# Starting the expert stage inside the attention's tail: last z, its output projection and a router among the first chunks, buffers laid out anew, big experts first

## The chip, the core and the metric

The kernel runs on one core of a Trainium2 chip. The metric is the device time of one execution in microseconds (us); the median of three runs is compared. The core's engines are TensorE (PE in the profile, which loads weights as PEld), VectorE (DVE), ScalarE (ACT), GpSimd (POOL) and SyncE (SP, which here only issues DMAs). Each runs its own list of instructions in order and waits on semaphores for the others.

## The reference

One transformer block with adaptive layer norms, for 4 batches of 512 positions and 256 features: causal attention with 16 heads of 128, then a feed-forward part with 8 experts, 2 of which each position uses.

```
h = _layernorm(x) * (1 + ca) + sa
x = x + ga * attention(h)              # q, k, v, causal softmax, output projection W_O
h = _layernorm(x) * (1 + cb) + sb
x = x + gb * ffn(h)

# ffn: HID = [128, 256, 384, 512, 128, 256, 384, 512]; gelu is the exact one
h      = x @ down_w + down_b                               # 256 -> 128
logits = x @ router_w + router_b - 1e-7 * cost
probs  = softmax(logits); topv, topi = top_k(probs, 2); gate = softmax(topv)
for k in range(2):                                         # every expert sees h times its mask
    acc = sum over e of gelu(gelu(h * mask[e]) @ w1 + b1) @ w2 + b2
    out = out + acc * gate[k]
out = out + 0.1 * (gelu(gelu(h) @ shared_w1 + shared_b1) @ shared_w2 + shared_b2)
out = out @ up_w + up_b + gelu(x) @ core_w + core_b
```

## The kernel before, in words

Two functions write out the whole program by hand as one list of events, `attention_plan()` and then `ffn_plan()`. Every engine walks this same list and issues, in its order, the instructions that are its own. So the list sets the order on every engine at once, and an event that an engine has to wait for holds up all that stands behind it on that engine. Every float32 product is made of three matmuls (L711 to L713) of a high and a low half: ACT writes the high half (a cast or an activation), DVE the low half (a subtraction that reads PSUM), and PE needs both.

The attention runs over 64 units (4 head groups x 4 batches x 4 heads; `NU` is 64). For unit u: **q/u**, **k/u** and **v/u** project, **S/u** makes the scores, **ri** and **norm** the softmax, **ty** transposes the probabilities on DVE (L1114 to L1117), **tr** moves them by DMA, **pt** splits them (casts on ACT, L681; two subtractions on POOL, L567), and **z/u** multiplies them by v. **wo/p/c** is the output projection of a pair of units (p from 0 to 31, two halves c): PE makes 12 matmuls of 256 columns, DVE scales into `fb` (L1127), POOL adds to X (L560).

Around it lie the events that prepare the second half for batch b: **st** and **nm** are the layer norm (**st/n**, **nm/n** with n = 4 + b, on DVE; its power of -0.5 on POOL, L507), **h2/b/k** transposes it on PE and ACT and DVE split it; **r/b** is the router's matmul (16 small ones, L832 and L833), **rs/b/1** to **rs/b/14** are the router's small steps on DVE (L947 to L981) with the exponentials **rp** on POOL (L542), and **wt/b** transposes the gates on PE (L890), after which SP stores them and **wl** loads each gate's row back, spread over the partitions. **dn/b** is the down projection with its gelu (`ur`), and **wh/n** splits a piece n of weights into W (cast on ACT, L628; subtraction on POOL, L552, or for the pieces in `BY_V`, 21 and 22 among them, on DVE, L1017).

The expert stage runs over 84 chunks, 21 for each batch t: chunk 0 is the shared expert, chunks 1 to 20 are blocks of 128 hidden units of the experts. Step n issues **w1/n** (PE into one of three S banks, gelu twice on ACT, L704 and L705, low half on DVE into `Gr`, L1241), then **w2/n-3** (PE accumulates into one of two T banks), then what the table `at` puts at this step. When the last chunk of an expert is through, **acc/t/e** multiplies by the gate on DVE (L1196, into `prod`) and adds on POOL (L533). w1/n waits for the low half of chunk n-3, and the first w2 of an expert waits for the acc of the expert two before it. At the turn of the batches **gx** (gelu of the features), **hs** (a POOL addition, L575), **up** and **D** are woven in.

The list ends its attention part with h2/1/1, S/63 and the rest of unit 63's softmax, z/61, then rs/0/13, rs/0/14, r/1, wt/0, wo/30/0, the statistics and normalisation of batch 2 (st/6, nm/6), z/62, dn/0, wo/30/1 and z/63. wo/31 stands in steps 1 and 2 of the expert stage.

The buffers of the attention (`qk`, `PB`, `vh`, `vl`, `pth`, `ptl`, `zt`) give their place to those of the expert stage (`ur`, `Gr` and so on), which are laid over them.

Of the kernel before, what the change touches and what calls it, by code (L numbers as in the profile page):

```python
# [44 lines left out]
def attention_plan():  # L45

    pre, post = {}, {}
    fill = {}

    def put(where, i, *events):  # L50
        where.setdefault(i, []).extend(events)

    put(post, 0, ("ms",))
    for b in (1, 2, 3):
        i = (0, 2, 5)[b - 1]
        if b == 1:
            put(pre, i, ("h", b, 0))
            put(post, i, ("h", b, 1))
            continue
        fill[i] = [[("st", b, 0)], [("st", b, 1)], [("st", b, 2)], [("st", b, 3)]]  # L60
        fill[i + 1] = [[("nm", b, 0)], [("nm", b, 1)]]
        put(post, i + 1, ("h", b, 0))
        put(post, i + 2, ("h", b, 1))
    for n in range(4, 16):
        put(pre, 16 * (n // 4 - 1) + 5 + 2 * (n % 4), ("wh", n))
    for n in range(16, 20):
        put(pre, 34 + n, ("wh", n))
    for b in range(2):
        fill[54 + 4 * b] = [[("st", B + b, k)] for k in range(4)]
        fill[55 + 4 * b] = [[("nm", B + b, 0)], [("nm", B + b, 1)]]  # L70
        put(post, 55 + 4 * b, ("h2", b, 0))
        put(post, 56 + 4 * b, ("h2", b, 1))
        put(post, 57 + 4 * b, ("r", b))
    fill[58] = [[("rs", 0, 1), ("rs", 0, 2)]] + fill[58]
    put(post, 58, *[("rp", 0, c) for c in range(4)])
    fill[59] += [[], [("rs", 0, 3)], [("rs", 0, 4)]]
    fill[60] = [[("rs", 0, k)] for k in range(5, 10)]
    fill[61] = [[("rs", 0, k)] for k in range(10, 15)]
    put(post, 61, ("wt", 0))
    fill[62] = [[("st", 6, 0), ("st", 6, 1)], [("st", 6, 2)], [("st", 6, 3)], [("nm", 6, 0), ("nm", 6, 1)]]  # L80
    put(post, 61, ("wh", 20), ("ld", 22))
    plan = [("mod0",)] + [("st", 0, k) for k in range(4)] + [
# [11 lines left out]
    for i in range(NU):  # L94
# [36 lines left out]
def ffn_plan():
# [12 lines left out]
    for k in range(3):
        put(0, 2 + k, ("d0", k))
    put(0, 4, ("h2", 2, 0))
    put(0, 5, ("h2", 2, 1), ("wl", 2), ("wl", 3))
    for k, j in enumerate((6, 7, 8, 9)):
# [12 lines left out]
    for b, n in ((1, 5), (2, 26), (3, 47)):  # L161
# [54 lines left out]
def build(nc, x, ct, wmod, wat, wfa, wfb, cst, bcol, b2, ub, cb, out, scr, scw):  # L216
# [20 lines left out]
    with ExitStack() as ctx:  # L237
# [33 lines left out]
        with ExitStack() as att:  # L271
# [14 lines left out]
        gob = sb("gob", 256)
# [145 lines left out]
        def _(sp):  # L432
# [16 lines left out]
            for ev in plan:  # L449
# [148 lines left out]
        def _(act):  # L598
# [15 lines left out]
            for ev in plan:  # L614
# [704 lines left out]
```

## Time and profile before

| | us |
|---|---|
| median of three runs | 830.65 (829.01 to 832.02) |
| the profiled execution | 829.57 |
| its span | 827.8 |
| PE busy | 796.7 (96%) |
| DVE busy | 675.7 (82%) |
| ACT busy | 629.1 (76%) |
| POOL busy | 448.9 (54%) |

The span is the time from the first to the last instruction that the profiler shows; the time of the execution has another 1.8 us around it. The attention ends and the expert stage begins at about 640 to 660 us of the span, and the last chunk ends at about 818 us.
### The profile page before, as it was taken

The numbers are of one execution on the slowest core, as the hardware profiler recorded it, in microseconds if no ns is written. First come the engines' busy times: TensorE is split into PE (matmuls) and PEld (weight loads), VectorE is DVE, ScalarE is ACT, GpSimd is POOL, SyncE is SP. The second block draws the span as 40 slices with busy tenths as digits, with TensorE's granted clock in tenths as the row PEclk, the third lists the DMA queues.
The fourth block names the chain that finished last, engine by engine and source line by source line (L and its number), as shares of the span: only waits on it lengthen the run. The fifth ranks groups of instructions, "written<-read, shape, count | busy, mean of one in ns | idle before, by whom it ended". The sixth has DMA issues, their size and how long they took to land.

```text
span 827.8 us, 14504 instructions
## 1 busy us (share of the span) xinstructions
PE 796.7 (96%) x4832; PEld 708.6 (86%) x4832; DVE 675.7 (82%) x1636; ACT 629.1 (76%) x1408; POOL 448.9 (54%) x310
## 2 busy tenths in 40 slices
PE   8899999999999999999999999999998698999997
PEld 7688888999999999999999999998997686788786
DVE  4779898888888888887888888889898778877776
ACT  3787878788877888778888788887777478686873
POOL 2555365654456556544566644675465554666753
PEclk8999999999999999999999999999999799999999
DMA  7252233342223443233233442244222220212131
GB/s 249 72 166 64 66 89 90 99 111 66 64 65 74 110 112 94 65 77 84 64 90 91 99 110 66 64 110 115 65 65 64 71 90 13 78 52 90 40 115 39
DMA packets 47593, 70.54 MB, mean 85 GB/s; under 512 B 5536, under 2 KB 38464, under 8 KB 47392
## 3 DMA queue, kind: packets, MB, share of 16 engines
q1 hardware_dynamic: 47008, 68.81, 31.5%
q0 software_dynamic: 368, 0.81, 0.4%
q8 instruction: 39, 0.64, 0.3%
q14 instruction: 34, 0.28, 0.1%
q10 hardware_dynamic: 144, 0.00, 0.0%
HBM read 25.49 MB, written 2.17 MB: 33 GB/s over the span
## 4 chain that ended last, share of the span: by engine, by line
PE 74%; ACT 11%; DVE 8%; issue 3%; POOL 2%; DMA 1%; SPq 0%; DVEq 0%; POOLq 0%; ACTq 0%
PE M L712 15%; PE M L713 15%; PE M L711 15%; PE S L711 6%; PE S L713 6%; PE S L712 6%; ACT PB L610 3%; PE T L711 2%; PE T L713 2%; PE T L712 2%; ACT PB L657 2%; DVE S L1098 2%; ACT qk L670 1%; ACT pth L681 1%; DVE gab L1114 1%
## 5 line engine op out<-in xcount | busy, mean ns | idle before, releaser
L610 ACT ACTIVATE PB<-S,nb 128x128 f32<-128x128 f32 (+3 forms) x256 | 133.8, 533 | 111.6 <-DVE nb L1098 111.6
L567 POOL TENSOR_TENSOR ptl<-ptl,pth 128x640 fp32r<-128x640 f32 x128 | 198.9, 1577 | 35.1 <-ACT pth L681 35.1
L560 POOL TENSOR_TENSOR X<-X,fb 128x512 f32<-128x512 f32 x64 | 83.2, 1301 | 245.5 <-DVE fb L1127 245.5
L1087 DVE TENSOR_TENSOR qk<-M,qk 128x512 fp32r<-128x512 f32 x128 | 88.4, 690 | 52.9 <-ACT qk L670 52.9
L657 ACT ACTIVATE PB<-PB,ri 128x256 f32<-128x256 f32 (+3 forms) x256 | 124.4, 580 | 5.4 <-DVE ri L1107 5.2
L1098 DVE CUSTOM_DVE_ANT_0 S<-S,cc 128x128 f32<-128x128 f32 (+3 forms) x256 | 117.6, 523 | 1.3 <-PE S L713 1.3
L1114 DVE STREAM_TRANSPOSE gab<-PB 128x256 f32<-128x256 f32 (+2 forms) x192 | 109.3, 623 | 0.3 <-DMA ptl<-gab 0.3
L711 PE MATMUL M<-hh,W 128*128 128x512 f32 x264 | 103.9, 394 | 1.2 <-DVE hl L1073 0.9
L712 PE MATMUL M<-hl,W 128*128 128x512 f32 x264 | 103.3, 391 | 0.0
L713 PE MATMUL M<-hh,W 128*128 128x512 f32 x264 | 103.2, 391 | 0.0
L681 ACT CAST pth<-ptl 128x640 fp32r<-128x640 f32 x128 | 87.6, 742 | 3.5 <-DMA ptl<-gab 3.5
L711 PE MATMUL S<-qk 128*128 128x128 f32 (+3 forms) x256 | 86.7, 339 | 3.4 <-DVE qk L1087 3.4
L704 ACT ACTIVATE Gr<-S,bc 128x512 fp32r<-128x512 f32 x84 | 58.5, 697 | 34.5 <-PE S L713 34.5
L712 PE MATMUL M<-ptl,vh 128*128 128x512 f32 (+3 forms) x256 | 83.1, 325 | 0.0
L1241 DVE TENSOR_TENSOR Gr<-S,Gr 128x512 fp32r<-128x512 f32 x84 | 57.4, 687 | 31.0 <-ACT S L705 29.0
L713 PE MATMUL M<-pth,vl 128*128 128x512 f32 (+3 forms) x256 | 82.7, 323 | 0.0
L713 PE MATMUL S<-qk 128*128 128x128 f32 (+3 forms) x256 | 82.6, 323 | 0.0
L712 PE MATMUL S<-qk 128*128 128x128 f32 (+3 forms) x256 | 82.4, 322 | 0.0
L711 PE MATMUL M<-pth,vh 128*128 128x512 f32 (+3 forms) x256 | 80.6, 315 | 1.5 <-DVE qk L1087 1.1
L670 ACT CAST qk<-M 128x512 fp32r<-128x512 f32 x128 | 76.1, 594 | 6.2 <-PE M L713 5.9
L711 PE MATMUL M<-W,hh 128*128 128x256 f32 x256 | 73.3, 286 | 4.1 <-DVE qk L1087 4.1
L712 PE MATMUL M<-W,hh 128*128 128x256 f32 x256 | 72.4, 283 | 0.0
(182 smaller groups left out, 2300.1 us busy)
## 6 DMA issues: line engine op xcount, KB each, us to landing
ptl<-gab SPq DMA_DIRECT2D x256, 160.0 KB, 3.1
stage<-in_wat SPq DMA_DIRECT2D x16, 512.0 KB, 5.0
gab<-scw SPq DMA_DIRECT2D x16, 256.0 KB, 3.3
tmp<-scw SPq DMA_DIRECT2D x16, 256.0 KB, 3.5
X<-in_x SPq DMA_DIRECT2D x3, 512.0 KB, 7.9
stage<-in_wfa SPq DMA_DIRECT2D x3, 512.0 KB, 4.7
out<-X SPq DMA_DIRECT2D x3, 512.0 KB, 2.6
X<-in_wmod SPq DMA_DIRECT2D x1, 1024.0 KB, 12.0
```

Source lines behind the costliest of these rows:

```text
L560: pool.tensor_tensor(X[:, a:a + 512], X[:, a:a + 512], fb[:, c2 * 512:c2 * 512 + 512], ALU.add).then_inc(s_y, 1)
L567: pool.tensor_tensor(ptl[u % 2][:, s], ptl[u % 2][:, s].bitcast(F32), pth[u % 2][:, s].bitcast(F32), ALU.subtract).then_inc(s_pl, 1)
L610: ins = act.activation(PB[:, P_OFF[i]:P_OFF[i] + w], PS[bk][:, a:a + w], ACT.Exp, bias=nb[:, i:i + 1], scale=-1.0, accum_out=sm[:, i:i + 1])
L657: act.activation(p, p, ACT.Copy, scale=ri[:, i:i + 1]).then_inc(s_P3, 1)
L670: act.copy(dst, src).then_inc(mh, 1)
L681: act.copy(pth[u % 2][:, s], ptl[u % 2][:, s].bitcast(F32)).then_inc(s_ph, 1)
L711: pe.matmul(o, lhs[0], rhs[0], start=start, stop=False, **kw)
L712: pe.matmul(o, lhs[0], rhs[1], start=False, stop=False, **kw)
L713: return pe.matmul(o, lhs[1], rhs[0], start=False, stop=stop, **kw)
L1087: v.tensor_tensor(lo, src, hi.bitcast(F32), ALU.subtract).then_inc(me, 1)
L1098: ins = v.tensor_tensor_reduce(PS[bk][:, a:a + w], PS[bk][:, a:a + w], mask[:, 512 - w:512], -INV, BIG, ALU.add, ALU.min, nb[:, i:i + 1])
L1114: v.transpose(Y_blocks(i, i + 1), P_blocks(i, 0, i + 1))
```

## The change

The end of the list is written anew. r/1, wt/0 and the last router steps leave the attention's tail; dn/0 comes straight behind z/61, then both halves of wo/30, z/62, the splitting of weight piece 21 and the last router steps of batch 0. pt/63, r/1, st/6, wt/0, z/63, nm/6, h2/2 and wo/31 stand in steps 0 to 7 of the expert stage. The splitting of piece 20 moves to before S/63. The layer norm of batch 3 (st/7, nm/7) stands one to three steps later, wt/1 one step later. The experts are taken in the order 3, 2, 1, 0, 4, 5, 6, 7, so that with 4, 3, 2 and 1 chunks they come first; weights and biases are packed in that order on the host. For the early start of `Gr` the halves of unit 62's and 63's probabilities are placed apart in memory, and `gob`, `ol`, `oh` and `prod` move behind `Gr`. What is computed is the same.

```
 ORDER = [3, 2, 1, 0, 4, 5, 6, 7]
 PLACE = [n for n, e in enumerate(ORDER) for _ in range(HID[e] // 128)]
...
-        put(post, 57 + 4 * b, ("r", b))
+    put(post, 57, ("r", 0))
...
-    fill[61] = [[("rs", 0, k)] for k in range(10, 15)]
-    put(post, 61, ("wt", 0))
-    fill[62] = [[("st", 6, 0), ("st", 6, 1)], [("st", 6, 2)], [("st", 6, 3)], [("nm", 6, 0), ("nm", 6, 1)]]
-    put(post, 61, ("wh", 20), ("ld", 22))
+    fill[61] = [[("rs", 0, 10)], [("rs", 0, 11)]]
+    put(post, 60, ("wh", 20))
...
-        if i + 2 == NU:
-            plan += [("dn", 0), ("b1",)]
-    return plan
+    last = NU // 2 - 2
+    plan += [("dn", 0), ("b1",), ("wo", last, 0), ("wo", last, 1), ("z", NU - 2), ("wh", 21), ("ld", 22)]
+    return plan + [("rs", 0, k) for k in range(12, 15)]
...
-    put(0, 0, ("wh", 21))
-    put(0, 0, ("rs", 1, 1))
-    put(0, 1, ("rs", 1, 2), ("wo", last, 0))
-    put(0, 2, ("wo", last, 1), ("wl", 0), ("wl", 1))
-    put(0, 3, ("wh", 22))
...
+    put(0, 0, ("pt", NU - 1))
+    put(0, 1, ("r", 1), ("st", 6, 0), ("st", 6, 1))
+    put(0, 2, ("wt", 0), ("wl", 0), ("st", 6, 2), ("st", 6, 3))
+    put(0, 3, ("wh", 22), ("rs", 1, 1), ("rs", 1, 2))
+    put(0, 4, ("z", NU - 1), ("nm", 6, 0), ("nm", 6, 1))
+    put(0, 5, ("h2", 2, 0), ("d0", 0))
+    put(0, 6, ("wo", last, 0), ("h2", 2, 1), ("d0", 1))
+    put(0, 7, ("wo", last, 1), ("wl", 1), ("wl", 2), ("wl", 3), ("d0", 2))
+    for k, j in enumerate((9, 10, 11, 11)):
         put(0, j, ("st", 7, k))
...
-    put(0, 12, ("dt",), ("nm", 7, 0))
-    put(0, 14, ("nm", 7, 1))
+    put(0, 12, ("dt",))
+    put(0, 13, ("nm", 7, 0))
+    put(0, 15, ("nm", 7, 1))
...
-        at_(n + 17 - (b == 1), ("wt", b))
+        at_(n + 17, ("wt", b))
```

How this moves instructions is shown at three places. The lines of the changed file lie 2 to 4 further down (L1241 is L1245 there). First VectorE in the attention's tail. Before, from the low half of v/31/1 (`vl`) on: router steps 12 to 14 of batch 0 (L975 to L981) stand on both sides of z/61's low half (`zt`), then follow r/1 (L942 to L945), the gates' copy of wt/0 (`rows`) and wo/30/0 (`fb`).

```order
L1087 TENSOR_TENSOR vl<-M,vh 128x512
L975 TENSOR_TENSOR rt<-cc,rt 128x32
L976 TENSOR_TENSOR rt<-cc,rt 128x32
L977 TENSOR_TENSOR rt<-rt 128x4
L1087 TENSOR_TENSOR zt<-M,zt 128x2x256
L979 TENSOR_TENSOR rt<-rt 128x32
L980 TENSOR_TENSOR rt<-rt 128x32
L981 TENSOR_TENSOR wg<-rt 128x32
```

In the change, from the same place on: z/61, dn/0 (`ur`), both halves of wo/30 (`fb`), z/62, weight piece 21 (`W`), and only then the six router instructions, ahead of the low halves of the first two chunks (`Gr`).

```order
L1091 TENSOR_TENSOR vl<-M,vh 128x512
L1091 TENSOR_TENSOR zt<-M,zt 128x2x256
L1231 TENSOR_TENSOR ur<-M,ur 128x512
L1131 TENSOR_TENSOR fb<-M,gab 128x512 x2
L1091 TENSOR_TENSOR zt<-M,zt 128x2x256
L1021 TENSOR_TENSOR W<-stage,W 128x1024
L979 TENSOR_TENSOR rt<-cc,rt 128x32
L980 TENSOR_TENSOR rt<-cc,rt 128x32
L981 TENSOR_TENSOR rt<-rt 128x4
L983 TENSOR_TENSOR rt<-rt 128x32
L984 TENSOR_TENSOR rt<-rt 128x32
L985 TENSOR_TENSOR wg<-rt 128x32
```

So z/61's low half no longer stands behind router steps, and the router steps stand behind z/62 and a weight piece. Second, VectorE in steps 13 to 15 of batch 0, where nm/7 makes the layer norm that h2/3/0 (PE, step 16) needs. Before, with S numbered, from the low half of w1/13 (S1) on: acc/0/4, w1/14, the second half of nm/7, rs/1/3 to 5, acc/0/5, w1/15.

```order
L1241 TENSOR_TENSOR Gr<-S1,Gr 128x512
L1196 TENSOR_TENSOR prod<-T0,tmp 128x512
L1241 TENSOR_TENSOR Gr<-S2,Gr 128x512
L1063 TENSOR_SCALAR stage<-X,mv,rs 128x256 x2
L952 TENSOR_REDUCE rt<-rt 128x4
L954 RECIPROCAL rt<-rt 128x4
L956 TENSOR_TENSOR rt<-rt 128x32
L1196 TENSOR_TENSOR prod<-T1,gab 128x512
L1241 TENSOR_TENSOR Gr<-S0,Gr 128x512
```

In the change, from the same low half on: the first half of nm/7, acc/0/4, w1/14, rs/1/3 to 5, acc/0/5, w1/15, and the second half of nm/7.

```order
L1245 TENSOR_TENSOR Gr<-S1,Gr 128x512
L1067 TENSOR_SCALAR stage<-X,mv,rs 128x256 x2
L1200 TENSOR_TENSOR prod<-T0,tmp 128x512
L1245 TENSOR_TENSOR Gr<-S2,Gr 128x512
L956 TENSOR_REDUCE rt<-rt 128x4
L958 RECIPROCAL rt<-rt 128x4
L960 TENSOR_TENSOR rt<-rt 128x32
L1200 TENSOR_TENSOR prod<-T1,gab 128x512
L1245 TENSOR_TENSOR Gr<-S0,Gr 128x512
L1067 TENSOR_SCALAR stage<-X,mv,rs 128x256 x2
```

The second half of nm/7 has moved behind four pieces of work that stood behind it before. Third, GpSimd in steps 29 to 35 of the stage (batch 1). Before: up/0/0 (X), rp/2/1, acc/1/3 (`stage`), up/0/1, two rp, then acc/1/4 and acc/1/5.

```order
L594 TENSOR_TENSOR X<-X,fb 128x512
L542 TENSOR_TENSOR rt<-ebase,rt 128x8
L533 TENSOR_TENSOR stage<-stage,prod 128x512
L594 TENSOR_TENSOR X<-X,fb 128x512
L542 TENSOR_TENSOR rt<-ebase,rt 128x8 x2
L533 TENSOR_TENSOR stage<-stage,prod 128x512 x2
```

In the change, from up/0/0 on: rp/2/1, up/0/1, acc/1/2, rp/2/2, acc/1/3, rp/2/3, then acc/1/4 and acc/1/5.

```order
L596 TENSOR_TENSOR X<-X,fb 128x512
L544 TENSOR_TENSOR rt<-ebase,rt 128x8
L596 TENSOR_TENSOR X<-X,fb 128x512
L535 TENSOR_TENSOR stage<-stage,prod 128x512
L544 TENSOR_TENSOR rt<-ebase,rt 128x8
L535 TENSOR_TENSOR stage<-stage,prod 128x512
L544 TENSOR_TENSOR rt<-ebase,rt 128x8
L535 TENSOR_TENSOR stage<-stage,prod 128x512 x2
```

Between up/0/1 and the last rp there are now two additions of experts, where there was none.

## Rows read from the trace of the kernel before

**Rows 1.** Busy time by stretch: stretch, length, PE, PEld, DVE, ACT, POOL, clock, DMA

```profile
640.00:650.00 10.00, 3.13 (x15) 2.91 (x16) 7.94 (x14) 3.67 (x6) 5.33 (x3) 0.51 0.29 67
...
690.00:700.00 10.00, 10.00 (x49) 8.03 (x48) 8.94 (x30) 9.58 (x17) 5.81 (x6) 1.00 0.09 25
...
720.00:740.00 20.00, 19.98 (x99) 16.41 (x98) 13.66 (x37) 15.31 (x26) 16.65 (x13) 1.00 0.21 66
```

**Rows 2.** Timeline of PE: start, length, what [idle time before it, its releaser]

```profile
38.25 0.33 PE L711 MATMUL S<-qk 128*128 128x128 f32 x1 [2.00 <-DVE qk L1087]
...
637.87 0.28 PE L832 MATMUL M<-W,hh 128*128 128x16 f32 x1 [0.88 <-DVE fb L1127]
...
646.87 1.01 PE L890 MATMUL M<-cc,wg 128*8 128x128 f32 x4 [7.05 <-DVE wg L981]
...
702.76 0.60 PE L890 MATMUL M<-cc,wg 128*8 128x128 f32 x4 [2.17 <-DVE wg L981]
```

**Rows 3.** Timeline of ACT in the tail

```profile
640.80 0.57 ACT L670 CAST zt<-M 128x512 fp32r<-128x512 f32 x1
...
654.93 0.65 ACT L689 ACTIVATE M<-M,bc 128x512 f32<-128x512 f32 x1
```

**Rows 4.** Timeline of PE: first matmuls of z/62, dn/0, wo/30/1 and w1/6

```profile
650.24 0.52 PE L711 MATMUL M<-pth,vh 128*128 128x512 f32 x1
...
652.24 0.45 PE L711 MATMUL M<-hh,W 128*128 128x512 f32 x1
...
653.69 0.28 PE L711 MATMUL M<-W,zt 128*128 128x256 f32 x1
...
670.07 0.48 PE L711 MATMUL S<-ur,W 128*128 128x512 f32 x1
```

**Rows 5.** Costliest groups: what, count, busy us, mean ns, idle time before

```profile
L1241 DVE TENSOR_TENSOR Gr<-S,Gr 128x512 fp32r<-128x512 f32 x84 | 57.4, 687 | 31.0 <-ACT S L705 29.0
```

**Rows 6.** Timeline of DVE in the tail: statistics of batch 2

```profile
651.09 1.39 DVE L1036 BATCH_NORM_STATS2 mv<-X 128x6 f32<-128x256 f32 x4
```

**Rows 7.** PE by single microseconds: stretch, length, busy time, clock, DMA

```profile
40.00:41.00 1.00, 1.00 (x6) 0.50 0.08 16
...
701.00:702.00 1.00, 0.00 (x0) 1.00 0.00 0
```

**Rows 8.** Timeline of POOL at four places

```profile
612.71 6.44 POOL L542 TENSOR_TENSOR rt<-ebase,rt 128x8 f32<-128x8 f32 x4
...
640.34 3.04 POOL L567 TENSOR_TENSOR ptl<-ptl,pth 128x640 fp32r<-128x640 f32 x2 [1.17 <-ACT pth L681]
...
688.88 1.30 POOL L533 TENSOR_TENSOR stage<-stage,prod 128x512 f32<-128x512 f32 x1 [3.87 <-DVE prod L1196]
...
728.54 3.24 POOL L542 TENSOR_TENSOR rt<-ebase,rt 128x8 f32<-128x8 f32 x2
```

**Rows 9.** Timeline of DVE beside that

```profile
613.31 0.73 DVE L1063 TENSOR_SCALAR tmp<-X,mv,rs 128x256 f32<-128x256 f32 x2
...
641.10 0.83 DVE L975 TENSOR_TENSOR rt<-cc,rt 128x32 f32<-128x32 f32 x1
...
689.52 1.13 DVE L1063 TENSOR_SCALAR stage<-X,mv,rs 128x256 f32<-128x256 f32 x2
...
726.07 0.68 DVE L1252 TENSOR_TENSOR fb<-M,gab 128x512 f32<-128x512 f32 x1
...
732.81 0.18 DVE L952 TENSOR_REDUCE rt<-rt 128x4 f32<-128x32 f32 x1
...
733.43 0.68 DVE L1196 TENSOR_TENSOR prod<-T,gab 128x512 f32<-128x512 f32 x1
```

**Rows 10.** Timeline of PE: w2/13, the first transpose of h2/3/0, w2/35

```profile
690.43 0.40 PE L711 MATMUL T<-Gr,W 128*128 128x512 f32 x1
...
691.13 0.60 PE L761 MATMUL M<-cc,stage 128*128 128x128 f32 x4
...
735.12 0.39 PE L711 MATMUL T<-Gr,W 128*128 128x512 f32 x1
```

More of the change, by code:

```diff
@@ L17 @@
 NC = sum(HID) // 128
-EXPERT = [e for e, h in enumerate(HID) for _ in range(h // 128)]
+ORDER = [3, 2, 1, 0, 4, 5, 6, 7]
+PLACE = [n for n, e in enumerate(ORDER) for _ in range(HID[e] // 128)]
 LAG = 3
@@ L93, in attention_plan @@
                 loads.setdefault(i + 1, []).append(ev[1] + 2)
-    for i in range(NU):
+    for i in range(NU - 2):
         steps = list(fill.get(i, []))
@@ L137, in put @@
         at.setdefault((t, j), []).extend(events)
-    put(0, 0, ("wh", 21))
-    put(0, 0, ("rs", 1, 1))
-    put(0, 1, ("rs", 1, 2), ("wo", last, 0))
-    put(0, 2, ("wo", last, 1), ("wl", 0), ("wl", 1))
-    put(0, 3, ("wh", 22))
[L144 to L148, printed above, removed]
+    put(0, 0, ("pt", NU - 1))
[7 more added lines that the diff above has]
+    for k, j in enumerate((9, 10, 11, 11)):
         put(0, j, ("st", 7, k))
@@ L204, in EXP_OF @@
     t, j = divmod(n, NC + 1)
-    return t, (0 if j == 0 else 1 + EXPERT[j - 1])
+    return t, (0 if j == 0 else 1 + PLACE[j - 1])
 MISC = {"h": True, "q": True, "k": True, "v": True, "z": True, "wo": False, "h2": True, "r": False,
@@ L276, in build @@
             PB = sa("PB", 1280)
+            pt0 = sa("pth0", 1280, F32R), sa("ptl0", 1280, F32R)
             vh, vl = sa("vh", 2048, F32R), sa("vl", 2048, F32R)
-            pth = [sa("pth0", 1280, F32R), sa("pth1", 1280, F32R)]
-            ptl = [sa("ptl0", 1280, F32R), sa("ptl1", 1280, F32R)]
+            pt1 = sa("pth1", 1280, F32R), sa("ptl1", 1280, F32R)
+            pth, ptl = [pt0[0], pt1[0]], [pt0[1], pt1[1]]
             zt = sa("zt", 2048, F32R)
@@ L282, in build @@
         Gr = sb("Gr", 4096, F32R)
+        gob = sb("gob", 256)
+        ol, oh = sb("ol", 512, F32R), sb("oh", 512, F32R)
+        sb("gap", 512)
+        prod = sb("prod", 1024)
         gxh, gxl = sb("gxh", 2048, F32R), sb("gxl", 2048, F32R)
-        oh, ol = sb("oh", 512, F32R), sb("ol", 512, F32R)
-        prod = sb("prod", 1024)
-        gob = sb("gob", 256)
         PS = [ctx.enter_context(nc.psum_tensor(f"S{n}", [128, 512], F32)) for n in range(3)]
@@ L423, in piece_after @@
                 return ("wo", 8 * (n // 4) - 9, 1)
-            return ("v", NU // 2 - 1, 1)
+            return (("q", NU - 1), ("k", NU - 1), ("v", NU // 2 - 1, 1))[n - 20]
         tmp_read = [use[("h", b, 1)] + 1 for b in range(B)] + [use[("h2", b, 1)] + 1 for b in range(B)]
@@ L465, in _ @@
                     if i < 2:
-                        sp.wait_ge(me, use[("wo", NU // 2 - 1, 1)] + 1)
+                        sp.wait_ge(me, use[("wo", NU // 2 - 5 + 4 * i, 1)] + 1)
                     elif i < 4:
@@ L470, in _ @@
                         sp.wait_ge(s_ac, acc_no[divmod(i - 4, 8)[0], (i - 4) % 8 + 1] + 1)
-                    sp.dma_start(wb_at(i), scw[i:i + 1, :].broadcast_to([128, 512])).then_inc(s_wb[i % 4], 16)
+                    row = i // 8 * 8 + ORDER[i % 8]
+                    sp.dma_start(wb_at(i), scw[row:row + 1, :].broadcast_to([128, 512])).then_inc(s_wb[i % 4], 16)
                 elif ev[0] == "tr":
@@ L702, in _ @@
                     bias = bc[:, B_SH1:B_SH1 + 1] if j == 0 else bc[:, B_B1 + j - 1:B_B1 + j]
+                    if n == 0:
+                        act.wait_ge(s_ty, NU)
                     act.wait_ge(s_f1, n + 1)
@@ L1279 @@
     wat = np.concatenate([perhead(A["L0_attn_W_Q"]), perhead(A["L0_attn_W_K"]), perhead(A["L0_attn_W_V"]), wo], 2)
-    wfa = np.concatenate([A[f"{f}e{e}_w1"] for e in range(8)] +
+    wfa = np.concatenate([A[f"{f}e{e}_w1"] for e in ORDER] +
                          [rowsplit(A[f + "down_w"]), rowsplit(A[f + "core_w"]), A[f + "shared_w1"],
                           A[f + "shared_w2"], A[f + "up_w"], rowsplit(A[f + "router_w"])], 1)
-    wfb = np.concatenate([rowsplit(A[f"{f}e{e}_w2"]) for e in range(8)], 1)
-    b1 = np.concatenate([A[f"{f}e{e}_b1"].reshape(-1, 128).T for e in range(8)], 1)
+    wfb = np.concatenate([rowsplit(A[f"{f}e{e}_w2"]) for e in ORDER], 1)
+    b1 = np.concatenate([A[f"{f}e{e}_b1"].reshape(-1, 128).T for e in ORDER], 1)
     bcol = np.concatenate([A[f + "down_b"][:, None], A[f + "shared_b1"][:, None], b1,
@@ L1290 @@
     cst[:, C_MASK + 384:C_MASK + 512] = np.where(np.tril(np.ones((128, 128))) > 0, 0, -1e10)
-    for c, e in enumerate(EXPERT):
-        cst[:, C_EXM + 8 * c:C_EXM + 8 * c + 8] = np.arange(8) != e
+    for c, n in enumerate(PLACE):
+        cst[:, C_EXM + 8 * c:C_EXM + 8 * c + 8] = np.arange(8) != ORDER[n]
     cst[:, C_IOTA:C_IOTA + 8] = np.arange(8)
```

## The prediction

> **What bounds the kernel now.** I read busy time by stretch first. TensorE is full almost everywhere; in the expert stage it is busy 19.98 of 20 us, and at the turn from attention to experts 3.13 of 10, at a clock of 0.51 [rows 1]. So a change in the order can win only where PE stands, and I went through PE's timeline for the stops. Around the turn they are 0.88 us before r/1 and 7.05 us before wt/0, and in step 21 of the experts 2.17 us before wt/1 [rows 2]. The long one has a plain cause: wt/0 waits for the last router step `wg` on DVE, and behind wt/0 in PE's own list stand wo/30, z/62, dn/0 and the first chunk, which need no gates yet. After the stop PE runs at half clock until about 650: the four transposes and the twelve matmuls of wo/30/0 take from 646.87 to 650.24, 3.37 us [rows 2, 4], where they need some 1.8 at full clock (1.45 for the twelve, below). Such a fall of the clock thus costs about 1.6 us.
>
> **The tail.** I rebuild the new tail on the old clock of the trace, from the end of z/61 (near 637) on, and compare when each kernel is ready to issue w1/6, which is 670.07 before [rows 4].
>
> dn/0 takes r/1's place and starts as r/1 did, at 637.87. It lasts 1.45 us (652.24 to 653.69 in rows 4; wo's twelve half-width matmuls make the same columns), so to 639.3. wo/30/0 needs z/61's low half: ACT's high half ends at 641.37 [rows 3], DVE needs 0.7 more, since the router steps that stood ahead of it are gone: 642.1. Two wo (2.9) and z/62 (2.0, rows 4) bring PE to 647.0. PE has stood 0.9 and 2.8 us so far. dn/0's activations, table load included, end on ACT 2.5 us after z/61's cast, DVE follows by 644.7, in time for z/62.
>
> From here PE has work of its own (two chunks, r/1, w1/2, wt/0, w1/3, w2/0, w1/4, w2/1, z/63, w1/5, w2/2), about 10.5 us with 0.5 of small waits, so to 658.0. Then h2/2/0 waits for nm/6, and nm/6 stands at the end of a DVE queue that I sum up. A 512-column subtraction takes 0.69, and one every 0.6 when they follow each other [rows 5]. z/62's low half ends at 648.5; weight piece 21 waits for ACT's cast (648.8) and takes 1.2: 650.1; six router steps 0.9: 651.0; chunk 0: 651.6; chunk 1 waits for ACT, which has made the cast, chunk 0 and pt/63 by then: 653.2; r/1's three steps, the last of them behind POOL's pt/63: 654.0; four statistics 1.39 [rows 6]: 655.4; chunk 2, the gates' copy, the rest of the statistics, chunk 3, half a weight piece, two router steps, acc/0/0, chunk 4 and z/63's low half, 5.0 together: 660.4; nm/6, four normalisations at twice the 0.73 of two [rows 9], 1.4 with overlap: 661.7. PE stands 3.7 us. After that it must still do h2/2/0, both halves of wo/31 and h2/2/1, 3.6 us, which before were done by 670.07: it is ready for w1/6 at 665.3. **Gain 4.75 us.**
>
> Moves that cost nothing there: weight piece 20 moves ahead of S/63, where ACT and POOL both wait for DVE's masks; its 1024 columns take POOL some 2.4 us (by the two halves of pt/62, 640 columns each, in 3.04, rows 8), and without that cover they would delay pt/62 by as much. The gate rows wl/1 to wl/3 are loaded only after wo/31/1 (near 671), and the first is wanted near 677. A `wg` that is caught behind POOL's pt/63 (it comes within 0.1 us of it) delays wt/0 by 1.5 us, but PE then waits less at h2/2/0; I take 0.2 at most.
>
> **The clock.** The new tail has two stops, 2.8 and 3.7 us. A stop of 2.00 us early in the trace was followed by half clock with PE full (0.50 at 40 to 41 us), one of 2.17 us in the expert stage was not (1.00 throughout) [rows 2, 7]. So each may cost 0 to 1.6. The second, longer one is nearer to the row that fell: I take 1.2, and 0.8 for the first. **Loss 2.0, bounds 0 and 3.2.**
>
> **Steps 12 to 16 of batch 0.** Here the change puts the second half of nm/7 behind four other things on DVE, and PE's h2/3/0 needs it. Before there was no slack to speak of: nm/7 ended at 690.65 [rows 9], PE reached h2/3/0 at 691.13 [rows 10]. In the same coordinates: the first half now stands ahead of acc/0/4 and w1/14, so that DVE is at 690.1 where the second half began (689.52). Of the three router steps the last waits for POOL's addition of acc/0/4 (1.30, rows 8; it starts 0.9 later than 688.88): 691.2. acc/0/5 to 691.9, w1/15's low half to 692.5, and now POOL is in acc/0/5's addition, until 693.2, and nm/7 waits for it. That DVE waits for POOL's current instruction is a thing that the trace shows: L975 took 0.83 us, where such a step takes 0.18 alone (L952), and ended as the first half of pt/62's subtraction did, and nm/7's own second half took 1.13 instead of 0.73 beside an addition [rows 8, 9]. nm/7 ends at 693.9, PE starts h2/3/0 at 694.0, 2.9 late. Behind it ACT was full before (9.58 of 10 us, rows 1) with the two h2, dn/1, two gx and five chunks up to wt/1, so the delay is handed on; wt/1 one step later gives back some 0.3 of its 2.17 us, since w1/22 had to wait for chunk 19 anyway. **Loss 2.6; 1.5 if nothing waits for POOL, 3.3 if each piece meets it.**
>
> **Batches 1 and 2, step 35.** rs/b/3 needs all four rp. Before, the last two ran back to back from 728.54 to 731.78 [rows 8] and DVE took rs/2/3 at 732.81 as soon as it came to it [rows 9]. Now POOL has the additions of acc/1/2 and acc/1/3 among them. up/0/1's addition cannot start before DVE's product ends at 726.75 [rows 9]; five instructions from there (three additions 1.3, two rp 1.62) end at 733.9. DVE stands until then, its third router step meets acc/1/4's addition until 735.2, and acc/1/5, which began at 733.43 [rows 9], ends at 736.0. w2/35 is the first of an expert that waits for it, and PE is there at 735.12 [rows 10]: 0.9 to 1.0 late. Batch 2 has the same order, batch 3 has no router. **Loss 2.0 for both, bounds 0 and 2.4.** Big experts first has no return here: PE had no stop at the head of a batch that the later acc could remove.
>
> **The sum.** -4.75 + 2.0 + 2.6 + 2.0 = +1.85 us on the profiled execution's 829.57, so 831.4. That execution lies 1.1 below the median of the runs (830.65), which the new kernel's median should also stand above: about 832.3, +0.2%. Under 0.3% is about what a measurement of this kernel cannot tell from no change.
>
> **Rivals.**
> - The clock decides (slower). The same losses, but both stops of the tail and the new one at h2/3/0 fall to half clock in full: 3.2 instead of 2.0, and up to 1.0 at h2/3/0, which ACT's queue there hides in part: +4.1, 834.7. It decides from the second full fall on. For it: two of the three stops are longer than the one that fell; against it: the one of 2.17 us that did not.
> - The gain holds (faster). The tail gains as worked out, less one fall, and the two later waits stay hidden, because DVE and POOL reach nm/7 and rs/b/3 with less behind them than before: -4.75 + 1.6 = -3.2 and less, 827.5. For it: DVE waited 31 us in all for ACT before the chunks' low halves [rows 5], and POOL is busy only 54%. Against: both waits are in order behind work that itself comes late.
> - Powers on POOL hold VectorE up (slower). The rule above: 1.3 more, 833.6. The row on the powers speaks against it; 0.03.
> - The change leaves the tail as it is. z/62 could still be late if POOL's pt/62 came later; it ends at 643.38 [rows 8] and PE wants it at 645: against.
>
> **How the numbers follow.** No measurable change, from 828.2 to 833.1: 0.47. Slower by more than 0.3% (the clock 0.35, the powers 0.03): 0.38. The gain holds: 0.15. The range takes the forecast's own with the slower rival up to its price and a microsecond, 828.2 to 835.7; outside remain most of the third case and a little of the slower, some 0.18.
>
> **What would show it.** In the changed profile: no stop at wt/0, z/62 near 645 instead of 650.24; stops of PE near 3 us before wo/30/0 and near 4 before h2/2/0, released by DVE; one of 2 to 3 us before h2/3/0, released by nm/7 (L1067 there); about 1 us at w2/35 and w2/56. I am wrong if PE meets h2/3/0 with nm/7 done, if rs/2/3 does not wait for POOL, or if DVE's queue in steps 0 to 4 ends well before or after 14 us from z/62.

## The result, and the profile after

| | before | after |
|---|---|---|
| median, us | 831.12 (829.01 to 832.96, 6 runs) | 836.73 (835.26 to 840.32, 6 runs) |
| the profiled execution | 829.57 | 837.1 |
| its span | 827.8 | 835.3 |

The changed kernel is slower: ratio 1.0076, interval 1.0050 to 1.0103, some 6 us. I had forecast no measurable change (832.3, range 828.2 to 835.7), so the time lies outside the range and on the side to which I gave 0.38. All ratios leave out executions more than 1.5% slower than the fastest of their kernel, which touches one run below, with two of its twelve.

The page of the changed kernel, its busy time and two of its forty-slice rows:

```profile
PE 803.0 (96%) x4832; PEld 711.0 (85%) x4832; DVE 673.4 (81%) x1636; ACT 628.8 (75%) x1408; POOL 449.4 (54%) x310
...
PE   8889999999999999999999999999998898999997
...
PEclk8999999999999999999999999999999969999999
```

PE is busy 6.3 us longer than before with no work added: a sign of matmuls that last longer. The clock's row has one 6, in the slice that ends near 689 us.

Three names are needed from here on. **dta/0** to **dta/2** are three groups of 14, 14 and 12 small matmuls, of 16 columns each, in steps 9 to 11 of batch 0. They read `g0z`, which three small steps on DVE make, **d0/0** to **d0/2**. **dt** in step 12 closes them with a few more small matmuls.

The timeline of PE after, at its stops and at the first matmul of two dta groups (start, length, what, idle time before it and its releaser):

```profile
642.00 0.36 PE L715 MATMUL M<-W,zt 128*128 128x256 f32 x1 [2.68 <-DVE zt L1091]
...
652.11 0.60 PE L894 MATMUL M<-cc,wg 128*8 128x128 f32 x4 [1.23 <-DVE wg L985]
...
661.50 1.09 PE L765 MATMUL M<-cc,tmp 128*128 128x128 f32 x4 [2.48 <-DVE tmp L1067]
...
672.84 0.25 PE L881 MATMUL M<-g0z,W 128*128 128x16 f32 x1 [0.45 <-issue]
...
674.39 0.48 PE L715 MATMUL S<-ur,W 128*128 128x512 f32 x1
...
676.81 0.21 PE L881 MATMUL M<-g0z,W 128*128 128x16 f32 x1
...
679.65 0.77 PE L715 MATMUL S<-ur,W 128*128 128x512 f32 x1
...
692.98 0.47 PE L715 MATMUL T<-Gr,W 128*128 128x512 f32 x1 [0.66 <-DVE prod L1200]
...
696.81 0.63 PE L765 MATMUL M<-cc,stage 128*128 128x128 f32 x4 [1.49 <-DVE stage L1067]
...
707.93 0.50 PE L715 MATMUL S<-ur,W 128*128 128x512 f32 x1 [1.65 <-DVE Gr L1245]
...
741.58 0.47 PE L715 MATMUL T<-Gr,W 128*128 128x512 f32 x1 [0.70 <-DVE prod L1200]
```

The 7.05 us before wt/0 [rows 2] are gone, and the forecast's new stops are there: 2.68 before wo/30/0, 2.48 before h2/2/0, 1.49 before h2/3/0, 0.70 before w2/35 (and again before w2/56). Three things are not in the forecast: a stop of 0.66 before w2/12, a stop of 0.45 ahead of dta/0, and the second dta group, which takes 2.84 us (676.81 to 679.65) where the first took 1.55 (672.84 to 674.39).

Busy time by stretch after (stretch, length, busy time of PE, PEld, DVE, ACT, POOL, granted clock, DMA):

```profile
672.00:674.00 2.00, 1.55 (x13) 1.19 (x11) 2.00 (x5) 1.43 (x3) 1.42 (x2) 1.00 0.11 42
674.00:676.00 2.00, 2.00 (x10) 1.66 (x10) 1.19 (x3) 0.23 (x1) 2.00 (x2) 0.69 0.87 294
676.00:678.00 2.00, 2.00 (x10) 1.81 (x8) 0.89 (x2) 1.01 (x2) 2.00 (x2) 0.50 0.71 188
678.00:680.00 2.00, 2.00 (x10) 2.00 (x10) 1.05 (x3) 0.00 (x0) 1.20 (x2) 0.50 0.03 8
680.00:682.00 2.00, 2.00 (x6) 1.52 (x6) 0.00 (x0) 0.69 (x2) 0.41 (x1) 0.50 0.44 131
682.00:684.00 2.00, 2.00 (x11) 1.90 (x9) 1.15 (x6) 0.55 (x2) 0.08 (x1) 0.50 0.00 0
684.00:686.00 2.00, 2.00 (x8) 1.81 (x8) 0.33 (x2) 0.00 (x0) 2.00 (x2) 0.50 0.00 0
686.00:688.00 2.00, 2.00 (x6) 0.86 (x5) 0.22 (x1) 1.24 (x2) 0.55 (x1) 0.50 0.00 0
688.00:690.00 2.00, 2.00 (x9) 1.33 (x9) 1.34 (x3) 0.44 (x1) 0.38 (x1) 0.90 0.00 0
```

From shortly after the first dta group to the end of dt, some 14 us, TensorE ran at half clock with PE busy 2.00 of 2. From 676 to 688 DVE and ACT are busy only 3.6 and 3.5 us of 12, so it is TensorE that sets the pace. Before, the same matmuls (675.75 to about 683) ran at 1.00:

```profile
672.00:676.00 4.00, 4.00 (x20) 3.25 (x19) 3.53 (x8) 3.99 (x8) 1.15 (x2) 1.00 0.56 193
676.00:680.00 4.00, 4.00 (x32) 3.72 (x31) 2.79 (x10) 1.73 (x3) 4.00 (x4) 1.00 0.25 94
680.00:684.00 4.00, 4.00 (x27) 3.54 (x27) 1.18 (x4) 1.31 (x3) 4.00 (x4) 1.00 0.13 41
```

The starts of chunks (w1/n) in the two traces, after less before, put on the same zero, the matmul behind the 0.9 us stop that both have (dn/0 at 637.66 after, r/1 at 637.87 before), give the account. Up to w1/9: -3.31. From w1/9 to w1/13, the steps of dta: +6.91 (the 0.45 stop with what goes with it 0.68; from w1/10 to w1/13 14.16 us where it was 7.93, so 6.23 for the clock). To w1/17: +2.33. To w1/25: -0.13. Step 35 of batch 1 +0.94, of batch 2 +0.96. Sum +7.7: the 7.5 by which the spans differ and the 0.21 of the zero. Without dta it would be +0.8, and the forecast was +1.85.

### The profile page after: what moved, and what is told of

It reads as the page before. It is cut to its first block, busy times and chain, and to the rows that moved or that the text cites. A ratio compares the mean times of both kernels' runs of the same rounds, so it can differ in the third digit from the quotient of the medians.

```text
span 835.3 us, 14505 instructions
## 1 busy us (share of the span) xinstructions
PE 803.0 (96%) x4832; PEld 711.0 (85%) x4832; DVE 673.4 (81%) x1636; ACT 628.8 (75%) x1408; POOL 449.4 (54%) x310
## 4 chain that ended last, share of the span: by engine, by line
PE 72%; ACT 13%; DVE 9%; issue 4%; POOL 2%; DMA 1%; SPq 0%; DVEq 0%; ACTq 0%; POOLq 0%
PE M L715 15%; PE M L716 15%; PE M L717 15%; PE S L715 6%; PE S L717 5%; PE S L716 5%; ACT PB L612 3%; ACT PB L659 2%; PE T L715 2%; PE T L716 2%; PE T L717 2%; DVE S L1102 2%; ACT pth L683 2%; ACT qk L672 1%; POOL rt L544 1%
## 5 line engine op out<-in xcount | busy, mean ns | idle before, releaser
L1245 DVE TENSOR_TENSOR Gr<-S,Gr 128x512 fp32r<-128x512 f32 x84 | 57.5, 687 | 33.9 <-ACT S L709 32.4
L715 PE MATMUL M<-W,hh 128*128 128x256 f32 x256 | 73.3, 286 | 4.1 <-DVE qk L1091 4.0
L715 PE MATMUL M<-W,zt 128*128 128x256 f32 x256 | 71.7, 280 | 2.7 <-DVE zt L1091 2.7
```

The costliest lines, as they stand in the source:

```text
L715: pe.matmul(o, lhs[0], rhs[0], start=start, stop=False, **kw)
```

## The experiments

**Theory A.** The loss is the half clock in dta: where a stop stands right ahead of these 40 matmuls of 16 columns, the clock falls among them, and it comes back only after they are done. **Rival B:** transfers or the engines that feed TensorE hold these steps, the clock only shows it. **Rival C:** the stop alone, or the narrow matmuls alone, do it. All ratios below are to the kernel before, on the same chip, with 95% intervals.

**The changed kernel again.** No edit.

> The changed kernel unaltered, beside the same runs of the kernel before as the next three, for the spread of its executions. In the kernels run so far an execution's time went with its mean granted clock: 827.8 at 0.996, 831.5 at 0.992, 833.5 at 0.988 with the d0 steps early. Theory A (narrow matmuls behind a stop bring the clock down): nearly all executions of the changed kernel at 0.986 or lower, at 835 to 840, median 836 to 837. Rival (the six executions seen so far had bad luck, and the kernels with d0 early or dta spread are not better): a spread from 828 to 838, median 832 to 833.

837.44 (8 runs), ratio 1.0067 (1.0039 to 1.0095). Single executions with their mean clock: 830.41 (0.992), 831.99 (0.992), 835.05 (0.988), then five from 837.42 (0.984) to 840.24 (0.980). With the first six, 12 of 14 executions took over 835 us. The loss came again, but it isn't in every execution: the profiled one was the fastest, with the stop and without the fall in dta (a row of PE's timeline, then PE's busy time and the clock by stretch):

```profile
672.23 0.25 PE L881 MATMUL M<-g0z,W 128*128 128x16 f32 x1 [0.92 <-issue]
```

```profile
670.00:674.00 4.00, 3.08 (x21) 1.00 0.22 40
674.00:678.00 4.00, 4.00 (x26) 1.00 0.63 226
```

The same program, 6.7 us faster than in the first profile, with PE at 1.00 in dta: w1/9 to w1/13 took 11.95 us where they took 17.73. A single trace without the fall is thus no proof that an edit removed it; the medians have to show that.

**Wide matmuls in dta.**

```diff
-  g = g0z[:, 16 * c:16 * c + 16]
-  pe.matmul(o[:, 0:16], w[0], g, ...)
+  g = g0z[:, 16 * c:min(16 * c + 128, 16 * NC)]
+  n = min(128, 16 * (NC - c))
+  pe.matmul(o[:, 0:n], w[0], g, ...)
... (w[1] alike)
```

> The changed kernel, but each of the 40 narrow matmuls of dta (16 columns) streams up to 128 columns; the extra columns land in a part of the PSUM bank that nobody reads, so the result is the same. Theory A (the clock): the changed kernel lost 6.2 us between w1/10 and w1/13 (14.16 us there, 7.93 before) because the granted clock fell to 0.50 while TensorE did little but narrow matmuls, and each of them cost twice the time. With wide ones the clock stays at 1.00, w1/10 to w1/13 takes 7.9 to 8.5, and the time is 830.5 to 831.5. Rival B (something else holds these steps: the weight transfers of 190 to 380 GB/s at 674 to 678, or the engines that feed TensorE, and the clock only shows it): the columns make no difference, 836.7. Rival C (the 0.45 us stop ahead of dta/0 sets the fall off): the fall comes all the same, but ends sooner; 833 to 836.

832.91, ratio 1.0024 (1.0003 to 1.0045), and in the profiled execution, the fastest of the twelve, w1/10 to w1/13 took 7.87 us at a clock of 1.00. Against rival B: nothing but the columns of these matmuls was changed, and some 4 us of the loss went. It is 1.4 to 2.4 more than I expected; the executions go from 828.3 (0.996) to 836.4 (0.986), so part of them still lose clock, where in the span isn't shown. The last matmuls of dta stay narrow here (96 to 16 columns) and the stop remains, 0.89 in this trace.

**Thinner groups.** `dta` in five groups of 8 at steps 9 to 13, `dt` at 15.

```diff
-    for c in range(3):
+    for c in range(5):
         put(0, 9 + c, ("dta", c))
-    put(0, 12, ("dt",))
+    put(0, 15, ("dt",))
...
-  for c in range(7 * ev[1], min(NC, 7 * ev[1] + 7)):
+  for c in range(4 * ev[1], 4 * ev[1] + 4):
...
```

> The changed kernel with dta in five groups of 8 matmuls at steps 9 to 13 instead of three of 14, 14 and 12 at steps 9 to 11, and dt at step 15 instead of 12. The same matmuls, thinner among the chunks. Theory A (the clock): fewer narrow matmuls at a time, no fall, w1/10 to w1/16 shorter by some 6 us: 830.5 to 832. If the density only matters little, half of it: 833.5. Rival B (transfers or feeding engines): as the changed kernel, 836.7.

830.61, ratio 0.9998 (0.9979 to 1.0016): as theory A has it. The same matmuls, the same stop (0.42 in this trace), but mixed with more chunks. Whether it or the wide matmuls do more the intervals don't tell.

**The stop taken away.**

```diff
-    put(0, 5, ("h2", 2, 0), ("d0", 0))
-    put(0, 6, ("wo", last, 0), ("h2", 2, 1), ("d0", 1))
-    put(0, 7, ("wo", last, 1), ("wl", 1), ("wl", 2), ("wl", 3), ("d0", 2))
+    put(0, 5, ("h2", 2, 0))
+    put(0, 6, ("wo", last, 0), ("h2", 2, 1))
+    put(0, 7, ("wo", last, 1), ("wl", 1), ("wl", 2), ("wl", 3))
+    for k in range(3):
+        put(0, 4 + k, ("d0", k))
```

> The changed kernel with the three DVE steps d0 one step earlier each (4 to 6 instead of 5 to 7), so that g0z is ready well before TensorE reaches dta/0 and the 0.45 us stop there is gone. Rival C (that stop sets the fall of the clock off): the clock stays at 1.00 through dta, 830.5 to 831. Theory A in the form that the narrow matmuls alone do it: dta starts 0.4 earlier, the clock falls all the same, 836 to 836.5.

831.76, ratio 1.0007 (0.9987 to 1.0026); twelve executions, 827.7 to 833.8, none below a clock of 0.988, where 11 of the changed kernel's 14 were. So the narrow matmuls alone don't do it: without the stop ahead of them the loss is gone. What the stop was, the page does not say ("issue"), but DVE's timeline of the changed kernel does:

```profile
671.22 0.69 DVE L1245 TENSOR_TENSOR Gr<-S,Gr 128x512 fp32r<-128x512 f32 x1 [0.32 <-ACT S L709]
671.82 0.68 DVE L1131 TENSOR_TENSOR fb<-M,gab 128x512 f32<-128x512 f32 x1
672.42 0.32 DVE L1153 TENSOR_TENSOR g0z<-g,g0z 128x160 fp32r<-128x160 f32 x1
```

L1153 is d0/2, the last of the three steps that make g0z. The change moved it from step 4 to step 7, behind wo/31/1 in DVE's list; it ends at 672.74, and dta/0 starts at 672.84.

PE in the kernel with d0 early, by stretch, dta included (the second fastest of the twelve executions):

```profile
668.00:672.00 4.00, 4.00 (x26) 1.00 0.11 22
672.00:676.00 4.00, 4.00 (x29) 1.00 0.80 247
```

**Dta later, and a stop put in, both in the kernel before.** First dta one step later:

```diff
-        put(0, 9 + c, ("dta", c))
-    put(0, 12, ("dt",), ("nm", 7, 0))
+        put(0, 10 + c, ("dta", c))
+    put(0, 13, ("dt",))
+    put(0, 12, ("nm", 7, 0))
```

> The kernel before with the three groups of dta one step later (steps 10 to 12, dt at 13). In the kernel before the same narrow matmuls ran at a clock of 1.00. Theory A, if it is the mere place of the groups in time that decides between full and half clock: a shift of 1.4 us can bring the fall here too, then 836 to 837; if before's surroundings (no stop and no fall of the clock in the 25 us ahead) protect it, 831. Rival B expects 831 as well.

830.60, ratio 1.0001 (0.9983 to 1.0019): with no stop ahead of it, dta one step later made no difference. Then dta where it was, and the last d0 late:

```diff
-    for k in range(3):
-        put(0, 2 + k, ("d0", k))
+    for k, j in enumerate((2, 3, 8)):
+        put(0, j, ("d0", k))
```

> The kernel before with one edit: the last d0 step at step 8 instead of 4, so that g0z comes late and TensorE stands some 0.3 to 1 us ahead of dta/0, as in the changed kernel. Theory A (a short stop right ahead of the narrow matmuls is what lets the clock fall through all of dta): the executions move from 827 to 834 to some 831 to 838, the median from 831 to 834 or 836, with clocks of 0.980 to 0.986; the profiled one may or may not show it. Rival (only the changed tail, with its own falls ahead, brings dta down): the stop alone costs its 0.3 to 1 us, 831.5.

837.29, ratio 1.0087 (1.0058 to 1.0116), above the 834 or 836 that I expected; all six executions above 836, at 0.974 to 0.982. This is the loss of the changed kernel without any of its changes: one small DVE instruction moved. The stop, 1.24 us, and the clock behind it (PE's timeline, then busy time by stretch with the clock after POOL's column):

```profile
677.31 0.25 PE L877 MATMUL M<-g0z,W 128*128 128x16 f32 x1 [1.24 <-issue]
```

```profile
676.00:680.00 4.00, 2.76 (x19) 2.53 (x19) 2.74 (x11) 0.65 (x2) 3.86 (x4) 0.93 0.27 72
680.00:684.00 4.00, 4.00 (x19) 3.71 (x17) 0.69 (x1) 1.24 (x2) 4.00 (x4) 0.50 0.24 63
...
688.00:692.00 4.00, 4.00 (x13) 2.96 (x14) 0.33 (x2) 1.24 (x2) 0.00 (x0) 0.50 0.00 0
```

w1/9 to w1/13 is 7.63 us longer than in the kernel before, and nothing after it moves (w1/83 is 7.68 later on the same zero). It tells against rival B too: here the tail, the order of experts and the transfers are those of before.

**The places of nm/7** (d0 early in this and all that follow).

```diff
-    put(0, 13, ("nm", 7, 0))
-    put(0, 15, ("nm", 7, 1))
+    put(0, 12, ("nm", 7, 0))
+    put(0, 14, ("nm", 7, 1))
```

> The changed kernel with d0 early (no fall of the clock in dta), and the two halves of nm/7 back at steps 12 and 14, where they stood before; the rest as changed. With d0 early alone TensorE stood 1.66 us before h2/3/0, and 0.66 before w2/12, and was 2.5 us later against the kernel before at w1/17 than at w1/15 (some 2.4 left at w1/25). If it is the place of nm/7 behind the router steps and acc/0/5 on DVE: that stop is gone, w1/25 comes 1.5 to 2.4 us earlier than with d0 early alone, time 1.5 to 2 lower, 829.5 to 830.5. If it is DVE's queue as a whole (the later acc of the big experts): the stop moves to another instruction behind and w1/25 gains under 0.7.

829.25, ratio 0.9984 (0.9968 to 0.9999), an interval that overlaps the one with d0 early alone; the trace is clearer. From w1/13 to w1/25 it takes 0.1 less than before, where with d0 early alone it took 2.39 more; the stops before w2/12 and h2/3/0 are both gone. nm/7's second half runs beside one of the router's exponentials on POOL (rp), not beside an addition, and takes 0.73 (DVE, then POOL):

```profile
689.29 0.73 DVE L1069 TENSOR_SCALAR stage<-X,mv,rs 128x256 f32<-128x256 f32 x2
```

```profile
688.50 1.65 POOL L546 TENSOR_TENSOR rt<-ebase,rt 128x8 f32<-128x8 f32 x1
```

In the changed kernel it stood behind the router steps and beside an addition on POOL, and took 1.30 (DVE, then POOL):

```profile
695.37 1.30 DVE L1067 TENSOR_SCALAR stage<-X,mv,rs 128x256 f32<-128x256 f32 x2
```

```profile
694.92 1.27 POOL L535 TENSOR_TENSOR stage<-stage,prod 128x512 f32<-128x512 f32 x1 [0.73 <-DVE prod L1200]
```

**Another order of experts.**

```diff
-ORDER = [3, 2, 1, 0, 4, 5, 6, 7]
+ORDER = [3, 0, 1, 2, 4, 5, 6, 7]
```

> The changed kernel with d0 early and the experts in the order 3, 0, 1, 2, 4 to 7 instead of 3, 2, 1, 0, 4 to 7. That puts POOL's additions of the second and third expert ahead of rp/2/1 and rp/2/2, none between rp/2/2 and rp/2/3 (in the changed order the third's stands there). If term d is right (rs/2/3 waits for rp/2/3, which stands behind these additions): the stop of 0.70 us before w2/35 and w2/56 is gone, and each of w1/39 and w1/60 gains 0.9: 1.9 us by the end, 830. If the product of the expert is late for another reason (ACT's queue, the gates): the stops stay. In batch 0 the additions come earlier as well, so the 0.66 before w2/12 should go too.

836.61 (834.96 for the ten executions in the ratio), ratio 1.0053 (1.0026 to 1.0081). Step 35 came out nearly as expected: w1/39 and w1/60 are 0.0 and 0.4 later than w1/38 and w1/59, not 0.9 each. The 0.66 before w2/12, which should have gone too, is still there in the trace. The time did not come out, since the second expert is now a single chunk: the third starts at w2/6 already and wants the PSUM bank of the first, whose product stands behind that of wo/31/1 on DVE (675.85, then 676.45 to 677.13). That is a new stop right ahead of dta (timeline of PE, then clock by stretch):

```profile
677.28 0.47 PE L717 MATMUL T<-Gr,W 128*128 128x512 f32 x1 [1.55 <-DVE prod L1202]
...
678.05 0.17 PE L883 MATMUL M<-g0z,W 128*128 128x16 f32 x1
```

```profile
676.00:680.00 4.00, 2.72 (x16) 0.84 0.44 165
680.00:684.00 4.00, 4.00 (x14) 0.50 0.55 162
684.00:688.00 4.00, 4.00 (x15) 0.50 0.23 69
```

I hadn't looked for that when I wrote the expectation. It repeats theory A in this trace with a stop that has another cause: g0z was ready (674.69 + 0.32), and still the clock fell. The same order with nm/7 back and dta in five groups:

> The changed kernel with d0 early, dta in five groups of 8, dt at 15, nm/7 at 12 and 14, and the experts in the order 3, 0, 1, 2, 4 to 7. If the terms add: relative to d0 early alone (831.8) 1.5 to 2.4 from nm/7 and 1.9 from the order, 827.5 to 828.5, below both kernels (before 830.9). If the stops only hand their time on to the next wait: 830 to 831.

832.04, ratio 1.0007 (0.9988 to 1.0026), a miss: the stop of 1.55 is there too, and the clock is low from 678 to 684 only (0.82, 0.50, 0.82 by two us). In this trace thinner groups make the fall short; they don't rule it out.

**Step 35 by the router's steps instead** (order of experts as changed, nm/7 back).

```diff
-  at_(n + 9 + (k - 3) // 3, ("rs", b, k))
+  at_(n + 9 + (k - 3) // 3 + (b > 1), ("rs", b, k))
```

> The changed kernel with d0 early and nm/7 back at steps 12 and 14 (829.25 us so far), and for batches 1 and 2 the router steps rs/b/3 to rs/b/9 one step later (36 to 38 of batch 1 instead of 35 to 37). Term d (rs/b/3 on DVE waits for rp/b/3 on POOL, and the product of the third expert's neighbour behind it comes late): the stop of 0.70 before w2/35 and w2/56 goes, w1/39 and w1/60 no later than w1/38 and w1/59, 0.9 each, time 827.4. If the late thing is the addition on POOL that the product's buffer waits for, and not DVE's wait: the stops stay, 829.2.

827.73, ratio 0.9970 (0.9949 to 0.9990), and the stops before w2/35 and w2/56 are gone (w1/39 and w1/60 0.0 later than w1/38 and w1/59). The interval overlaps that of the kernel without this edit, so the gain is read from the trace. So DVE's wait was it, as the changed kernel's DVE shows (rs/2/3 waits for rp/2/3, the expert's product follows behind two more steps):

```profile
739.63 0.19 DVE L956 TENSOR_REDUCE rt<-rt 128x4 f32<-128x32 f32 x1 [1.15 <-POOL rt L544]
...
740.76 0.68 DVE L1200 TENSOR_TENSOR prod<-T,gab 128x512 f32<-128x512 f32 x1
```

**TensorE kept at work in the tail's stops** (nm/7 back, router steps as changed).

```diff
+  if ev == ("wo", NU // 2 - 2, 0):
+      warm(30)
...
+  if ev == ("h2", 2, 0):
+      for _ in range(20):
+          pe.matmul(o[:, 0:128], Dz[:], Dz[:], start=True, stop=True)
```

> The changed kernel with d0 early and nm/7 back, and TensorE kept at work in the two stops of the tail: 30 matmuls of 128 columns on zeros ahead of wo/30/0, 20 ahead of h2/2/0, into PSUM banks free at that time (nothing reads them). Term b (a fall of the clock after each stop, in part of the executions, some 1.5 us each): mean granted clock of the executions at 0.990 and above instead of 0.985 to 0.993, the slower half of the spread gone, median 828 to 828.5 instead of 829.25. If the stops' falls are hidden by DVE, which ends last there anyway: same median, 829.2; if the extra matmuls themselves run past the data they fill the time for: up to 1 us slower.

828.69, ratio 0.9970 (0.9951 to 0.9990). No execution was below a clock of 0.990 (0.985 without), but the medians, 828.69 and 829.25, can't be told apart by their intervals: inconclusive on the time. In the profiled execution the clock held at both stops and fell at a third, the 1.23 before wt/0, which was left as it was. The filling isn't exact there: 1.72 us of the first stop were left ahead of the 30 matmuls, and wo/30/0 came 5.03 us behind dn/0, where it came 4.34 behind it without them.

**All of it:** d0 early, nm/7 back, router steps later, matmuls in the stops, dta in five groups.

> The changed kernel with d0 early, nm/7 back, the router steps of batches 1 and 2 one step later, the matmuls in the two stops, and dta in five groups with dt at step 15. If the four add up: 826 to 827, 0.5% below the kernel before. If dta in five groups takes back a little in batch 0 (it did nothing for the median with a stop ahead of it removed): 827 to 828.

824.67 (7 runs, 822.28 to 828.26), ratio 0.9939 (0.9910 to 0.9968): 6 us below the kernel before, 12 below the changed one, and 1.3 below what I expected. In the trace w1/83 comes 4.3 us earlier than before on the same zero; where the rest of the 6 us comes from isn't shown.

## Why the prediction was wrong

The sum was right but for one term. (By its own figures its median is 832.5, 831.4 and 1.1, and not 832.3; nothing rests on that.) Point by point:

- **The tail, -4.75.** With d0 early, no fall of the clock showed in the tail of the profiled execution, and w1/9 came 4.67 us earlier than before. h2/2/0 was to start at 661.7 and started at 661.50 (661.71 on the zero of before); the two large stops were to be 2.8 and 3.7, and were 2.68 and 2.48. The 1.23 before wt/0 was named in the forecast (`wg` caught behind POOL's pt/63) and set at 0.2, since PE waits that much less at h2/2/0, as it did.
- **The clock, +2.0, bounds 0 and 3.2: the step that failed.** It read: "The new tail has two stops, 2.8 and 3.7 us. [...] So each may cost 0 to 1.6." In the tail it was not far off: in the profiled execution none at the first stop and 1.36 at the second (4.67 less 3.31); in four later profiles the clock fell at the first. But it looked for falls only behind the two long stops, and took the price of a fall from a place with wide matmuls behind it (3.37 instead of 1.8 us). The fall that decided came in dta, behind 0.45 us, and cost 6.23. I had not followed d0 in DVE's list, so its move from step 4 to step 7 had no place in the sum; and I had no price for a fall among matmuls of 16 columns, during which the clock did not come back here. The trace of before could have made me look: r/1 has 16 such matmuls, and the clock fell right behind them (PE busy until 639.8, clock 0.75 in 640.0 to 640.5 and 0.50 from there; 0.51 over 640 to 650 [rows 1]). It doesn't prove it, since the 7.05 us of the stop begin there as well, and in the trace with the late d0 the same fall came only 1.9 us into the stop.
- **Steps 12 to 16, +2.6.** 2.33 lost by w1/17 and 0.13 given back by w1/25: 2.2. The place was right (nm/7 behind the queue on DVE, undone by moving it back), and the addition that stretches it too; the wait shows as 0.66 before w2/12 and 1.49 before h2/3/0, not as one of 2.9.
- **Batches 1 and 2, +2.0.** 0.94 and 0.96. Right in place, cause and size. "Big experts first has no return here" was wrong in one respect: with a small expert second, the first one's PSUM bank is wanted back while wo/31/1 is still on DVE, and PE stood 1.55 us.
- **The rivals.** "The clock decides (slower)" named the right engine and the right sign, at the wrong place: 834.7 by falls in the tail and at h2/3/0. The h2/3/0 stop brought no fall in that trace (1.00 from 690 on). "The gain holds" was wrong in its condition: neither later wait stayed hidden (2.2 and 1.9). "Powers on POOL hold VectorE up" did not come: the first half of nm/7 took 0.73 us while such a power (rp) ran on POOL (changed kernel, DVE, then POOL):

```profile
691.51 0.73 DVE L1067 TENSOR_SCALAR stage<-X,mv,rs 128x256 f32<-128x256 f32 x2
```

```profile
690.86 1.64 POOL L544 TENSOR_TENSOR rt<-ebase,rt 128x8 f32<-128x8 f32 x1
```

None of the three signs by which I said I would be wrong came: all three watched places that were in the sum.

What stays open: why two of fourteen executions of the changed kernel stay under 832 us at 0.992, with a stop of 0.92 in the one that was profiled; and why, in terms of TensorE, a short stop counts ahead of narrow matmuls. A stop ahead of narrow matmuls decides whether most executions lose the clock, not whether a single one does.

## What to carry to other kernels

When a change moves steps, follow the small ones too, and ask of each what TensorE does in the microseconds behind it: with wide matmuls behind it a stop of 0.89 us cost 1.1 us in one trace here (w1/9 to w1/13), while with 40 narrow ones one of 0.45 cost 6.9. Make the inputs of narrow matmuls early, or spread them among wide ones. And take a second look at a kernel that "loses" after a change: here five small edits turned 0.7% slower into 0.6% faster.

## What the runs showed that I had not expected

- A busy PE can stay at half clock. From 676 to 688 us PE was busy 2.00 of 2 in every row and the clock stayed at 0.50; it came back near 688.4, when a chunk and dt had run behind the last narrow matmul (684.9). The Trainium skill (TensorE: Matmul & The Clock Gate, section Part 1: The HAM clock gate) says that the clock is set by how busy TensorE has been. By the profile's busy time the trace does not agree: 2.00 of 2, at 0.50.
- The time of an execution goes with its clock. With d0 early, twelve executions: 827.7 to 828.1 us at 0.996, 831.2 to 831.8 at three of 0.992, 832.5 to 833.2 at 0.990, 833.7 and 833.8 at 0.988; one, 829.2 at 0.991, doesn't fit. An execution 0.004 lower has 6.6 us more at half clock (0.004 of 828, twice), and took some 3.7 longer: about half of it. The kernel before spread as much, from 827.1 to 834.0, so that twelve runs beside 24 to 35 of before leave an interval of 0.4%, and steps of 1 us are read from the traces. There, too, only times on the same zero compare: in the fourteen profiles that zero itself lies between 635.85 and 641.95.
- A wait that the profile calls "issue" can be a plain wait for another engine: the 0.45 ahead of dta/0 ended 0.1 us after d0/2 did, and so did the 1.24 in the kernel before with the late d0 (677.31 and 677.21).
